# High and low parts in tiles of their own, and contractions over 64 rows, in a 32-sequence transformer kernel

## The reference, cut to what matters

```python
def reference(x, ...):                       # x: 32 sequences, 256 positions, 128 features
    h = relu(conv(x))                        # 8 taps, 128 -> 64 features, 248 positions are left
    y = layernorm(h)
    q, k, v = y @ Wq.T + bq, y @ Wk.T + bk, y @ Wv.T + bv
    prob = softmax(q @ k.T * 64**-0.5)       # rows with q[0] == 0 or k[0] == 0 give 0
    h = h + (prob @ v) @ Wo.T + bo
    y = layernorm(h)
    w = softmax(top2(y @ Wg + bg + bias))    # 8 experts, the two best get weights
    return h + sum(w[e] * (relu(y @ W1[e] + b1[e]) @ W2[e] + b2[e]) for e in range(8))
```

## Time and profile before

| | |
|---|---|
| median of 3 runs (lowest, highest) | 343.15 us (342.94, 343.67) |
| span of the profiled execution | 340.8 us |
| median less that span: what lies around it | 2.35 us |
| PE matmul busy | 307.6 us (90%) |
| DVE busy | 248.6 us (73%) |
| ACT busy | 240.9 us (71%) |
| mean granted TensorE clock | 0.959 |

### The profile page before, as it was taken

How to read it: one execution, slowest core, us unless ns; L and a number is a source line. 1 busy time by engine, 2 the same in 40 slices (tenths; PEclk the granted TensorE clock), 3 DMA queues, 4 the chain that set the end, 5 groups by cost and what they waited for, 6 DMA issues and landing times.

```text
span 340.8 us, 6412 instructions
## 1 busy us (share of the span) xinstructions
PE 307.6 (90%) x1486; PEld 188.0 (55%) x1486; DVE 248.6 (73%) x824; ACT 240.9 (71%) x545; POOL 92.8 (27%) x85
## 2 busy tenths in 40 slices
PE   8587799999999999999999999999999999979754
PEld 8264657565645657475656556474656565534220
DVE  2574747879696979779786969697887979492823
ACT  2427497969686887879686978778786969764520
POOL 1103031513232241515122322315151323132302
PEclk9767899999999999999999999999999999999985
DMA  6120214070614225160706142241707060504050
GB/s 181 50 61 0 63 58 124 17 182 5 159 37 124 73 78 119 29 168 5 191 1 151 45 130 67 81 116 26 171 9 187 2 164 0 147 21 126 12 136 15
DMA packets 17228, 28.38 MB, mean 83 GB/s; under 512 B 3264, under 2 KB 13760, under 8 KB 17216
## 3 DMA queue, kind: packets, MB, share of 16 engines
q1 hardware_dynamic: 16928, 27.98, 32.6%
q10 hardware_dynamic: 288, 0.28, 0.2%
HBM read 21.90 MB, written 2.29 MB: 71 GB/s over the span
## 4 chain that ended last, share of the span: by engine, by line
PE 40%; DVE 22%; issue 16%; ACT 11%; DMA 7%; SPq 1%; DVEq 1%; ACTq 0%; POOL 0%
PE bank_a L787 11%; DMA cb<-weights 5%; DVE ts L252 4%; PE bank_y L846 4%; PE bank_s L897 4%; PE bank_h L836 3%; PE bank_h L837 3%; ACT p L367 3%; ACT hid L376 2%; PE bank_b L904 2%; PE bank_s L804 2%; DVE hsum L637 2%; DVE acc L548 2%; DVE gw L617 2%; PE bank_h L867 2%
## 5 line engine op out<-in xcount | busy, mean ns | idle before, releaser
L376 ACT ACTIVATE hid<-bank_h,col 128x496 f32<-128x496 f32 x128 | 84.0, 674 | 10.5 <-PE bank_h L837 9.2
L846 PE MATMUL bank_y<-hid,w_sb 128*64 128x496 f32 x256 | 68.0, 612 | 3.6 <-DVE acc L548 3.6
L836 PE MATMUL bank_h<-xs,w_hi 128*128 128x496 f32 x128 | 56.2, 439 | 3.0 <-DVE xs L253 2.4
L548 DVE SCALAR_TENSOR_TENSOR acc<-bank_y,col,cb 128x496 f32<-128x496 f32 x64 | 45.4, 730 | 17.3 <-DMA cb<-weights 9.8
L837 PE MATMUL bank_h<-xs,w_lo 128*128 128x496 f32 x128 | 49.8, 389 | 0.0
L262 POOL TENSOR_TENSOR total<-acc 128x496 f32<-128x496 f32 x16 | 20.1, 1256 | 106.7 <-DVE acc L548 106.7
L330 POOL TENSOR_TENSOR p<-p,rmask 124x496 f32<-124x496 f32 x32 | 32.4, 1014 | 51.9 <-DVE rmask L564 51.8
L265 POOL TENSOR_TENSOR total<-total,acc 128x496 f32<-128x496 f32 x16 | 20.0, 1250 | 70.5 <-DVE acc L548 70.5
L836 PEld LDWEIGHTS bank_h<-xs,w_hi 128*128 128x128 f32 x128 | 24.3, 190 | 13.4 <-issue 7.1
L718 DVE SCALAR_TENSOR_TENSOR h<-bank_s,col,h 128x248 f32<-128x248 f32 x16 | 7.6, 476 | 31.9 <-PE bank_s L897 31.9
L367 ACT ACTIVATE p<-bank_s,nmax 124x248 f32<-124x248 f32 x64 | 29.4, 466 | 0.3 <-DVE nmax L555 0.2
(11 more groups left out here) (105 smaller groups left out, 584.8 us busy)
## 6 DMA issues: line engine op xcount, KB each, us to landing
cb<-weights SPq DMA_DIRECT2D x64, 248.0 KB, 4.5
kk<-kk SPq DMA_DIRECT2D x16, 248.0 KB, 2.9
x<-xt SPq DMA_DIRECT2D x15, 256.0 KB, 2.9
out<-h SPq DMA_DIRECT2D x16, 124.0 KB, 1.8
w_sb<-w SPq DMA_DIRECT2D x3, 256.0 KB, 3.6
wtok_sb<-wtok SPq DMA_DIRECT2D x1, 256.0 KB, 2.7
x<-xt ACTq DMA_DIRECT2D x1, 256.0 KB, 3.9
weights<-ct_sb SPq DMA_DIRECT2D x16, 15.5 KB, 1.4
```

What stands on the lines that cost most here:

```text
L376: act.activation(hid[2 * (p % 2) + s][:, :], bank_h[s][:, 0:TOK], ACT.Relu, bias=col[:, C_B1 + e:C_B1 + e + 1]).then_inc(hid_ready[s], 1)
L548: dve.scalar_tensor_tensor(out=acc[p % 2][:, :], in0=bank_y[p % 2][:, 0:TOK], scalar=col[:, C_B2 + p:C_B2 + p + 1], in1=cb[:, p, :], op0=A ...
L836: pe.matmul(bank_h[e % 2][:, 0:TOK], w1_hi[:, e, :], xs[par][:, :], start=True, stop=False)
L846: last = pe.matmul(bank_y[p % 2][s * D:s * D + D, 0:TOK], w2_sb[:, 2 * p + s, :], hid[2 * (p % 2) + s][:, :], start=True, stop=True)
```

## The change

Each high and each low part gets a tile of its own, 128 x 248, with both sequences in their halves of the rows. Scores and `hidden` are then three products (high x high, high x low, low x high) of 64 rows and 248 columns for each sequence; the sequences take turns, one in rows 0 to 63 and one bank, one in rows 64 to 127 and another bank. `hidden` fills both banks with every expert, so expert e+1 waits for the `relu` of expert e. `queries_keys` takes block-diagonal weights and six matmuls of 248 columns. The two score blocks become one, and the key copy is gone. The lists of PE and ACT are reordered.

```diff
@@ PE: scores, hidden, queries_keys
-                pe.wait_ge(k_copied, 16 * n + 16)
+                parts = ((q_hi, k_hi), (q_hi, k_lo), (q_lo, k_hi))
                 for i in range(2):
-                    for part in range(2):
-                        last = pe.matmul(bank_s[b][0:HALF, i * WIN:(i + 1) * WIN],
-                                         qs[:, b * WIN + i * HALF:b * WIN + (i + 1) * HALF],
-                                         kk[:, part, b * WIN:(b + 1) * WIN], start=(part == 0), stop=(part == 1))
+                    for k, (q, key) in enumerate(parts):
+                        for b in range(PAIR):
+                            last = pe.matmul(bank_s[b][0:HALF, i * WIN:(i + 1) * WIN],
+                                             q[of_seq(b), i * HALF:(i + 1) * HALF], key[of_seq(b), :],
+                                             start=(k == 0), stop=(k == len(parts) - 1))
...
-                after(pe, hid_ready[e % 2], 4 * m + e // 2)
-                pe.matmul(bank_h[e % 2][:, 0:TOK], w1_hi[:, e, :], xs[par][:, :], start=True, stop=False)
-                pe.matmul(bank_h[e % 2][:, 0:TOK], w1_lo[:, e, :], xs[par][:, :], start=False,
-                          stop=True).then_inc(l1_done, 1)
+                after(pe, hid_ready[(e - 1) % 2], 4 * m + (e + 1) // 2)
+                parts = ((w1_hi, xs_hi), (w1_hi, xs_lo), (w1_lo, xs_hi))
+                for k, (w, xp) in enumerate(parts):
+                    for b in range(PAIR):
+                        last = pe.matmul(bank_h[:, b, 0:WIN], w[of_seq(b), e, :], xp[par][of_seq(b), :],
+                                         start=(k == 0), stop=(k == len(parts) - 1))
+                last.then_inc(l1_done, 1)
...
-                pe.matmul(bank_b[:, 0:TOK], wqk_hi[:, :], ts[:, :], start=True, stop=False)
-                pe.matmul(bank_b[:, 0:TOK], wqk_lo[:, :], ts[:, :], start=False, stop=True).then_inc(qk_done, 1)
+                parts = ((wqk_hi, xn_hi), (wqk_lo, xn_hi), (wqk_hi, xn_lo))
+                for which in range(2):
+                    for k, (w, xp) in enumerate(parts):
+                        last = pe.matmul(bank_b[:, which * WIN:(which + 1) * WIN], w[:, which, :], xp[:, :],
+                                         start=(k == 0), stop=(k == len(parts) - 1))
+                last.then_inc(qk_done, 1)
@@ ACT and DVE: high and low parts, one instruction for each
-                    high_parts(ts, xn).then_inc(thi, 1)
+                    act.activation(xn_hi[:, :], xn[:, :], ACT.Copy).then_inc(thi, 1)
-                    low_parts(dve, ts, xn).then_inc(tlo, 1)
+                    dve.tensor_tensor(xn_lo[:, :], xn[:, :], xn_hi[:, :].bitcast(F32),
+                                      ALU.subtract).then_inc(tlo, 1)
@@ SP: gone
-                    sp.dma_start(kk[0:D, :, :].bitcast(F32), kk[D:128, :, :].bitcast(F32)).then_inc(k_copied, 16)
```

More of the change, by code:

```diff
@@ L110, in audio_tower @@
         xn2 = sb("xn2", [128, WIN])
[L111 to L114, removed]
+        xn_hi = sb("xn_hi", [128, WIN], F32R)
+        xn_lo = sb("xn_lo", [128, WIN], F32R)
+        xs_hi = [sb(f"xs_hi{i}", [128, WIN], F32R) for i in range(2)]
+        xs_lo = [sb(f"xs_lo{i}", [128, WIN], F32R) for i in range(2)]
+        q_hi = sb("q_hi", [128, WIN], F32R)
+        q_lo = sb("q_lo", [128, WIN], F32R)
+        k_hi = sb("k_hi", [128, WIN], F32R)
+        k_lo = sb("k_lo", [128, WIN], F32R)
         v_sb = sb("v_sb", [128, 2, VCOLS])
@@ L375, in relu @@
                 after(act, y_done, 4 * m + p - 1)
-                act.activation(hid[2 * (p % 2) + s][:, :], bank_h[s][:, 0:TOK], ACT.Relu,
+                act.activation(hid[2 * (p % 2) + s][:, :].rearrange("p (b t) -> p b t", b=PAIR),
+                               bank_h[:, :, 0:WIN], ACT.Relu,
                                bias=col[:, C_B1 + e:C_B1 + e + 1]).then_inc(hid_ready[s], 1)
@@ L414, in high_queries_keys @@
                 act.wait_ge(qk_done, c + 1)
[L415 to L418, removed]
+                after(act, sc_done, c)
+                act.activation(q_hi[:, :], bank_b[:, 0:WIN], ACT.Identity, bias=col[:, C_BQ:C_BQ + 1])
+                act.activation(k_hi[:, :], bank_b[:, WIN:TOK], ACT.Identity, bias=bks[:, :]).then_inc(qkh_ready, 1)
             act.wait_ge(par_conv, 16 * N_CONV)
@@ L438, in iteration @@
                     act.activation(x_hi[:, :, :], x_sb[odd][:, :, :], ACT.Copy).then_inc(xh_ready, 1)
+                if n_:
+                    turned(n, 0)
+                if m_:
+                    relu(m, 3)
                 if c_:
@@ L449, in iteration @@
                     high_queries_keys(c)
+                if m_:
+                    relu(m, 5)
                 if n_:
@@ L452, in iteration @@
                 if m_:
-                    relu(m, 5)
+                    relu(m, 6)
                 if n_:
                     rsqrt(n, 1, bank_s[0], xn2_ready)
+                if m_:
+                    relu(m, 7)
                 if d_:
@@ L460, in iteration @@
                     after(act, l1_done, 8 * (n - 1))
-                    high_parts(xs[odd], xn2).then_inc(xhi, 1)
-                if m_:
-                    relu(m, 6)
+                    act.activation(xs_hi[odd][:, :], xn2[:, :], ACT.Copy).then_inc(xhi, 1)
                 if d_:
@@ L530, in expert_parameters @@
                 dve.tensor_copy(w1_hi[:, :, :], w1_sb[:, :, :]).then_inc(set_dve, 1)
-                dve.wait_ge(set_dve, 5)
+                dve.wait_ge(set_dve, 6)
                 dve.tensor_tensor(w1_lo[:, :, :], w1_sb[:, :, :], w1_hi[:, :, :].bitcast(F32),
                                   ALU.subtract).then_inc(set_dve, 1)
[L535 to L541, removed]
             def weigh(m, p):
@@ L866, in _ @@
             for _ in range(WARMUP):
-                pe.matmul(bank_h[0][:, 0:128], warm[:, :], warm[:, :], start=True, stop=True)
+                pe.matmul(bank_h[:, 0, 0:128], warm[:, :], warm[:, :], start=True, stop=True)
             pe.wait_ge(set_conv, 2)
@@ L937, in iteration @@
                     turn_p(n, 0)
+                if m_:
+                    hidden(m, even, 3)
                 if f_:
                     fold_halves(f)
-                if m_:
-                    expert_out(m, 1)
                 if n_:
@@ L944, in iteration @@
                 if m_:
+                    expert_out(m, 1)
                     hidden(m, even, 4)
@@ L953, in iteration @@
                     attend(n)
-                if d_:
-                    conv(d, range(2, 4))
                 if m_:
@@ L958, in iteration @@
                 if d_:
-                    conv(d, range(4, 6))
+                    conv(d, range(2, 6))
                 if n_:
@@ L962, in iteration @@
                     centre(n, 1, bank_s[0], h2[odd])
+                if m_:
+                    hidden(m, even, 6)
                 if d_:
@@ L968, in iteration @@
                     values(c)
+                if m_:
+                    expert_out(m, 2)
+                    hidden(m, even, 7)
                 if d_:
                     conv(d, range(10, 12))
-                if m_:
-                    hidden(m, even, 6)
-                    hidden(m, even, 7)
                 if n_:
@@ L983, in iteration @@
                     last.then_inc(gate_done, 1)
-                if m_:
-                    expert_out(m, 2)
                 if c_:
-                    scores(c, 0)
+                    scores(c)
                 if n_:
```

76 lines of the change are left out of this document (32 added, 44 removed).

## The result

The changed kernel takes **387.15 us** (median of 4 runs, 385.15 to 388.39), the kernel before, run beside it, 343.41 us: a ratio of 1.1246 [1.1205, 1.1287], 44 us slower. The profiled execution took 386.43 us with a span of 384.2. The forecast was 381 with a range of 349 to 405.

The account below looks back on a forecast made before the run. PE's list and its waits were taken as the bound. 340.8 + 39.9 (13 iterations of -0.83 + 2.55 + 1.35 = 3.07) - 4 + 2 = 378.7 us of span, 381 us in all, range 349 to 405.

Parts of the forecast that it names:

- a ring of vector engines: Rival: the chain of waits through DVE and ACT sets the period, about 315 us; chance 0.05 for under 342.5.
- (a): PE's streaming in hidden, scores and queries_keys, two sequences at once in the row halves: -0.83 us an iteration.
- halves in turn: Rival: the two halves of the rows run one after the other, 0.115 us more a pair, 431 us; chance 0.13.
- (b): PE's 23 changes of tile shape an iteration, at 0.15 into a column block and 0.20 into others: together +2.55 us.
- (c): PE's scores wait behind DVE's logits, as hidden 7 and expert_out 2 moved ahead of the conv: +1.50 us an iteration.
- (d): hidden 1 on PE waits 0.35 us for the relu of expert 0, turn_weights 0.2 more, each iteration.
- (e): Less work on ACT and DVE, near 2 us an iteration, covered by PE's list and so counted as nothing.
- The start: The key copy, once on the chain at the start for 4.0 us, is gone: -4 us.
- The clock: Rival: the 1.5 us waits before the scores let the granted clock fall, time over 400 us; chance 0.03.
- the ends: Iterations at both ends, with changes of shape but without the wait for the logits: some 2 us more.

Follow-up runs that it names:

- scores-only kernel: The kernel before with only the changed queries, keys and scores and no key copy; hidden stays stacked, the order kept: 339.81 us, 0.9858.
- conv first: The changed kernel with the last two conv matmuls ahead of expert_out 2 and hidden 7, relu 7 behind late and xs_hi: 361.81 us, 1.0494.
- full shapes: hidden as three products of 128 rows and 248 columns, mixing the sequences: 374.32 us against the changed kernel, 348.38 us with the conv first.
- all parts first: The changed kernel with DVE's logits and low part of xs ahead of both_taps, ACT's xs_hi ahead of late: 379.9 us, 1.1051.

## Why the prediction was right, and where its numbers were off

**Direction and bound: right.** PE's list and its waits set the time; the rival in which a ring of vector engines was the bound fell. The cleaner evidence is the scores-only kernel, which keeps the order: DVE has 3.7 us less work in a pass there (26.7 for 30.4), and the pass is 0.2 us shorter.

**(a) Streaming: right.** Pairs at 0.11, in either order of the list; the rival of halves in turn fell with that.

**(b) Changes of shape: the price right, the sum too high.** At a single block it holds. In the third pass a centre, hidden 6 and two conv matmuls take from 206.01 to 207.62, 1.61 us, of which 0.41 + 0.345 + 0.47 is streaming: 0.385 for two changes, where 0.40 was reckoned. The rule that a change of tiling drains the array (the Trainium skill, TensorEngine Tiling (Array Packing), Key Properties) is what these rows show: 0.78 without a load before a 64-row block. But removing nine of them gives 0.8 and 0.95 us an iteration (13 us in two runs) and not 1.8: counted net they are worth half. Waits that come back explain a third of the missing half.

**(c) The wait for the logits: right, and the main cause.** 1.55 us measured, 1.50 predicted, by the same chain of late, hsum and lg. The conv's earlier place, with relu 7 behind late, is worth 25 us, and the changed order with the old hidden makes a loss as large as the whole. The shares of order and form don't simply add: hidden's new form costs nothing in the changed order, and with the conv first its changes of shape cost 13 us.

**(d) One buffer for hidden: right in size.** Hidden 0's streaming ended at 148.93 (its last pair started at 148.81) and hidden 1 loaded at 149.94, 1.01 us later, of which PE's own work fills 0.71: a wait of 0.30 for 0.35. The load for turn_weights waits 0.5 us in total over the four iterations, 0.13 each, for the predicted 0.2.

Together these gave 3.07 us an iteration and 2.6 was measured at full clock. No row that I read holds the 0.47 between; the net worth of the changes of shape is where I would look.

**(e) Lighter vector engines at 0: near it, the exact size open.** With the order kept, the scores alone gain 1.4%. The thirteen iterations take 240.9 us there for 243.2, or 0.2 less each, where the expectation's terms for PE (-0.23 + 0.24 + 0.20) make 0.2 more; so, as an estimate, everything else together is worth 0.4 us an iteration and not 2. How this divides between lighter vector work and traffic is open.

**The start: the term that failed.** "Gone: -4" measured +0.1 at the first mark, and the first scores start 0.3 sooner. The copy stood on the chain, but just behind it stood the logits. In the changed kernel's timeline of PE at the first scores:

```profile
39.98 0.38 PE L794 MATMUL bank_s<-k_hi,q_hi 64*124 64x248 f32 x2 [0.82 <-DVE lg L572]
```

Before, the first scores started at 40.30 with the copy; without it they wait for lg and start at 39.98. I took the length of a link of the chain for its slack against the next arrival.

**The clock: counted at nothing, with 0.03 for a fall that takes the time above 400 and 0.01 for a small one.** The small one came: six stretches in the loop cost 4.8 us. Two of them began in the last 0.3 us of the wait before the scores, some 1.55 us long, and four 1.3 to 1.6 us after the scores had started. One of them, PE in the changed kernel, at 1.2 GHz from the first row on:

```profile
256.37 0.57 PE L794 MATMUL bank_s<-k_hi,q_hi 64*124 64x248 f32 x2 [1.56 <-DVE lg L572]
256.74 0.41 PE L794 MATMUL bank_s<-k_lo,q_hi 64*124 64x248 f32 x2
256.95 0.41 PE L794 MATMUL bank_s<-k_hi,q_lo 64*124 64x248 f32 x2
```

Pairs are 0.21 apart there instead of 0.11. Not every such wait is followed by a fall: the third pass has two waits and none, and the kernel with full shapes in the changed order has eleven waits of 1.63 us on average between 106 and 327 us and no fall there. The two kernels with waits of at most 0.6 at this place (all parts first, conv first) had none in the loop. I varied waits and never the clock alone, so that they cause the falls is argued, not shown.

**The sum.** Too high: the loop at full clock (39.9 for 33.8). Too low: the start (-4 for +0.1), the clock (0 for 4.8), the first two iterations (0 for 1.0) and the ends (2 for 3.7). They partly cancel: 38 us predicted, 43.4 measured. That the total came within 6 us owes something to luck; the direction and the size of the wait don't.

**Open.** 348 us with the conv first and full shapes is still 8 above the scores alone at 340, where hidden 6, 7 and the other blocks keep their old places. New hidden in the wholly old order wasn't tried: both banks are taken there by one expert.

## What to carry to other kernels

Before moving work in an in-order list, name what it was covering: the chain from the last conv matmul to the logits needed 2 us of other matmuls behind it, and putting two blocks back there gave 25 of the 44 us. A removed link of the chain is worth only the time until the next arrival at the same instruction; work removed from a loop is worth only what the waits behind it don't take back. Split a compound edit and time its parts: the half of this one that asked for no new order was a gain.

## What I had not expected of the hardware

- Matmuls in different halves of the rows ran in pairs even where the list had the three of one half ahead of the three of the other (389.03 us against 387.15).
- The granted clock fell to 0.50 six times in a loop whose longest waits were 1.7 us. In the loop before it stayed at 1.00, and in the loops of the two kernels whose waits at the scores and behind them were 0.6 and less too. But it also stayed at 1.00 through eleven waits of 1.63 us on average (full shapes, changed order, 106 to 327 us).
- Nine changes of shape cost the same 13 us in a list with a long wait (387.15 to 374.32) and in one without (361.81 to 348.38).
